# Graph attention and a routed feed-forward layer on one core: TensorE's program in loops, rows fetched by a transposing transfer, half of the rounded halves from ScalarE, small weights in three transfers

## The reference

```python
x = x + gnn(layernorm(x), adj, W, a)     # 4 heads of 32; softmax over connected nodes
x = x + ffn(layernorm(x), Wg, bg, W1, b1, W2, b2)
# gnn: h = x @ W; e = leaky_relu(s1[n] + s2[m]); attention = softmax(e where adj); attention @ h
# ffn: 8 experts of 128 -> 512 -> 128 with relu; each token goes to its 2 best by gate score,
#      weighted by the softmax of the two scores
```

## Time and profile before

| | |
|---|---|
| median of 3 runs | 625.47 us (624.49 to 626.54) |
| the profiled execution | 624.53 us, its span 622.6 us |
| mean granted TensorE clock | 0.928 |
| busy: TensorE, VectorE, ScalarE, GpSimd | 477.3, 515.9, 447.7, 402.5 us |
| line 1369, sums over neighbours | 3072 matmuls, 131.1 us |
| line 1560 and line 1543, the experts | 1704 matmuls, 107.6 us; 852 matmuls, 107.1 us |
| line 673, relu | 284 activations, 137.3 us, 0.563 each |
| line 662, copy of the transposed rows | 71 activations, 42.4 us |
| line 519, outputs written | 142 transfers, 170.1 us of GpSimd, 1.198 each |

### The profile page before, as it was taken

One profiled execution on the slowest core, in us unless ns is written; L12 is line 12 of the kernel. 1 busy time (PEld: TensorE's weight loads), 2 busy tenths in 40 slices (PEclk: granted clock), 3 DMA queues, 4 the chain that ended last, 5 costly groups with the idle time before them and its releaser, 6 DMA issues.

```text
span 622.6 us, 22344 instructions
## 1 busy us (share of the span) xinstructions
PE 477.3 (77%) x7450; PEld 435.4 (70%) x7509; DVE 515.9 (83%) x1619; ACT 447.7 (72%) x908; POOL 402.5 (65%) x342
## 2 busy tenths in 40 slices
PE   0687887977888787988867866799999999997000
PEld 0576787867888777988766755688888888887000
DVE  4689998999999999999988984678788888886297
ACT  1585778878888888998717745678888888884264
POOL 2241235887777777787776787878778887887300
PEclk9997999889989999999896998999999999999555
DMA  8922221222222233231113252233333323331499
GB/s 312 399 107 68 70 70 34 73 98 96 95 75 64 93 106 99 96 100 37 37 45 83 76 147 78 79 90 89 88 88 93 88 79 91 86 86 37 136 367 307
DMA packets 60781, 67.92 MB, mean 109 GB/s; under 512 B 7267, under 2 KB 46318, under 8 KB 60417
## 3 DMA queue, kind: packets, MB, share of 16 engines
q1 hardware_dynamic: 41936, 44.31, 22.9%
q0 software_dynamic: 8816, 17.46, 8.4%
q10 hardware_dynamic: 9920, 4.73, 2.6%
HBM read 44.16 MB, written 23.22 MB: 108 GB/s over the span
## 4 chain that ended last, share of the span: by engine, by line
issue 31%; DVE 29%; POOL 15%; PE 9%; DMA 8%; ACT 6%; POOLq 1%; SPq 1%; DVEq 0%; ACTq 0%
POOL expert_out L519 13%; PE bank L1369 4%; DVE edge L816 4%; DVE bs L719 3%; ACT xn L575 3%; DVE G L824 3%; DMA G<-in_L_ffn_W 2%; PE bank L1360 2%; DVE mv L722 2%; DMA adji<-expert_out 2%; POOL expert_rows L469 2%; DVE T L833 2%; DVE rowt L863 1%; DVE sc L759 1%; DMA G<-expert_out 1%
## 5 line engine op out<-in xcount | busy, mean ns | idle before, releaser
L519 POOL DMA_INDIRECT expert_out<-late,bidx x142 | 170.1, 1198 | 43.3 <-issue 42.7
L469 POOL DMA_INDIRECT expert_rows<-rowt,idx x128 | 156.6, 1223 | 40.6 <-issue 35.7
L570 ACT ACTIVATE G<-bank,s2c 128x512 uint8<-128x512 f32 x256 | 153.7, 703 | 0.0
L673 ACT ACTIVATE late<-bank,b1s,sc 128x256 f32<-128x256 f32 x284 | 137.3, 563 | 13.0 <-PE bank L1543 12.5
L1369 PE MATMUL bank<-V,G 128*128 128x66 bf16 x3072 | 131.1, 198 | 4.0 <-ACT G L570 0.5
L1369 PEld LDWEIGHTS bank<-V,G 128*128 128x128 fp8e4 x3072 | 121.0, 100 | 8.8 <-issue 1.6
L1560 PE MATMUL bank<-W2h,G 128*128 x1704 | 107.6, 220 | 20.2 <-DVE late L1239 18.7
L1560 PEld LDWEIGHTS bank<-W2h,G 128*128 128x128 f16 x1704 | 97.4, 98 | 36.2 <-issue 35.8
L1543 PE MATMUL bank<-late,W1h 128*128 128x256 f16 x852 | 107.1, 277 | 0.0
L1224 DVE TENSOR_TENSOR G<-late,G 128x1024 f16<-128x1024 f32 x71 | 87.0, 1226 | 2.4
L1543 PEld LDWEIGHTS bank<-late,W1h 128*128 x852 | 81.6, 99 | 9.1
(11 more groups left out here) (166 smaller groups left out, 688.9 us busy)
## 6 DMA issues: line engine op xcount, KB each, us to landing
adji<-in_adj SPq DMA_DIRECT2D x16, 1024.0 KB
V<-expert_rows SPq DMA_DIRECT2D x71, 130.0 KB
adji<-expert_out SPq DMA_DIRECT2D x8, 512.0 KB, 5.8
G<-expert_out SPq DMA_DIRECT2D x8, 512.0 KB, 8.4
expert_out<-late,bidx POOLq DMA_INDIRECT x142
G<-in_L_ffn_W SPq DMA_DIRECT2D x1, 2048.0 KB, 13.4
late<-in_L_ffn_W SPq DMA_DIRECT2D x1, 2048.0 KB, 10.1
expert_rows<-rowt,idx POOLq DMA_INDIRECT x128
```

The costliest lines, as they stand in the source:

```text
L469: pool.indirect_dma_start(xs, bass.IndirectOffsetOnAxis(ap=idx[:, Z.q, k, j:j + 1], axis=0), rowt[:, Z.q, j, :], None).then_inc(scattered[ ...
L519: pool.indirect_dma_start(ybuf, bass.IndirectOffsetOnAxis(ap=bidx[:, B.o, t:t + 1], axis=0), ysb[:, B.q, t, :], None, bounds_check=2 * TOK ...
L570: act.activation(Gs[:, M.p, h // 2, mt, :, h % 2], zb[h][:, :], ACT.Sign, bias=s2c[:, M.p, mt, h:h + 1]).then_inc(S["z_used"], 1)
L673: act.activation(h32[:, U.p, c, :], Up[U.p][c // 2][:, (c % 2) * BLK:(c % 2 + 1) * BLK], ACT.Relu, bias=b1s[:, bass.ds(ex * NC + c, 1)], s ...
```

## The change

- TensorE's slots 6 to 15 and its blocks' steps 17 to 64 run in hardware loops, two slots and eight steps per round. Waits in a loop have values computed from the loop's counter. The expert numbers come up to ten per load instead of one per block.
- SP loads a block's rows by a transposing transfer straight into `xt` (now four buffers), and the two index columns by a second transfer. TensorE's transposes, the PSUM copy on ScalarE and their semaphores go.
- ScalarE makes six activations per block: the four into `h32`, and chunks 2 and 3 once more, directly in half precision into the high half. VectorE makes the high half of chunks 0 and 1 alone, by a reduction over one element instead of a cast; the difference waits for all six.
- The small weights come in three transfers on ScalarE's queue, with W's transpose and the gate's made on the host; two transposes on TensorE and two copies go. VectorE casts most constants after the first shift. The first group's inverse deviation comes before the bias loads on GpSimd.
- `products` makes all four small products first and signals them by themselves; `scores` waits for these alone.
- Statistics of groups 2 and on come one slot later, the largest value of W1 at the end of slot 0, and the adjacency of graph 1 is loaded ahead of the rest of x.

```diff
+LOOP_SLOT = 6
+LOOP_STEP = SHARED + 1
+UNROLL = 8
+LOOPS = (BLOCKS - 2 - LOOP_STEP) // UNROLL
+REDUCED = 2
+HID_STEPS = NC + NC - REDUCED
...
             def load_rows(B):
-                ge(sp, S["bt_ready"], B.n - 3)
+                ge(sp, S["up_ready"], (B.n - 3) * NC)
                 ge(sp, S["bidx_ready"], B.n - 3)
                 r = sp.value_load(tab[0:1, 0, bass.ds(B.n, 1)], min_val=0, max_val=E * CAP)
-                sp.dma_start(xb[:, B.q], xs[bass.ds(r, BLK), :].rearrange("(t p) w -> p t w", p=P)) \
+                sp.dma_start(xt[:, B.q], xs[bass.ds(r, BLK), 0:D].bitcast(FP16), transpose=True) \
+                  .then_inc(ld_rows[B.q], 16)
+                sp.dma_start(xb[:, B.q], xs[bass.ds(r, BLK), D:ROW].rearrange("(t p) w -> p t w", p=P)) \
                   .then_inc(ld_rows[B.q], 16)
...
-            for k in range(2):
-                for h in range(H):
-                    lo = HD * (1 - k)
-                    act.dma_start(acol[HD * h:HD * (h + 1), k:k + 1],
-                                  a[h:h + 1, lo:lo + HD].rearrange("h d -> d h")).then_inc(S["ld_small"], 16)
+            act.dma_start(acol[:, :], a).then_inc(S["ld_small"], 16)
+            act.dma_start(WW[:, :, :], W).then_inc(S["ld_small"], 16)
+            act.dma_start(Wgr[:, :], Wg).then_inc(S["ld_small"], 16)
...
-                if X:
-                    act.wait_ge(S["bt_ready"], X.n + 1)
-                    ge(act, S["up_ready"], (X.n - 1) * NC)
...
-                    act.activation(xt[:, X.p], XTp(X), ACT.Copy).then_inc(S["xt_ready"], 1)
...
+                    ge(act, S["down_ready"], U.n - 3)
+                    for c in range(REDUCED, NC):
+                        act.activation(hp[:, U.q, 0, c], Up[U.p][c // 2][:, (c % 2) * BLK:(c % 2 + 1) * BLK],
                                        ACT.Relu, bias=b1s[:, bass.ds(ex * NC + c, 1)], scale=sc[:, 10:11]) \
                            .then_inc(S["hid_ready"], 1)
...
-                dve.wait_ge(S["hid_ready"], U.n * NC + NC)
+                dve.wait_ge(S["hid_ready"], U.n * HID_STEPS + REDUCED)
                 ge(dve, S["down_ready"], U.n - 3)
                 c = Chain(dve, S["split_steps"], 2, U.n)
-                c.did(dve.tensor_copy(hp[:, U.q, 0], h32[:, U.p]))
+                c.did(dve.tensor_reduce(hp[:, U.q, 0, 0:REDUCED], h32[:, U.p, 0:REDUCED].unsqueeze(3), AX.X, ALU.max))
+                dve.wait_ge(S["hid_ready"], U.n * HID_STEPS + HID_STEPS)
                 c.wait()
                 c.did(dve.tensor_tensor(hp[:, U.q, 1], h32[:, U.p], hp[:, U.q, 0], ALU.subtract))
...
                 for j in range(NT):
-                    mm(HP[:, j * P:(j + 1) * P], xnT[:, j * P:(j + 1) * P], Wr[:, :], start=True, stop=True)
                     last = mm(s12p[:, j, :], xnT[:, j * P:(j + 1) * P], Wa[:, :], start=True, stop=True)
+                last.then_inc(S["s12_ready"], 1)
+                for j in range(NT):
+                    last = mm(HP[:, j * P:(j + 1) * P], xnT[:, j * P:(j + 1) * P], WW[:, 0, :], start=True, stop=True)
                 last.then_inc(S["h_ready"], 1)
...
+            with pe.Fori(0, (NB - LOOP_SLOT) // 2) as i:
+                body(at_slot(LOOP_SLOT, i))
+                body(at_slot(LOOP_SLOT + 1, i))
...
+            def load_experts(n, where, count):
+
+                _, values = nc.values_load_multi_w_load_instructions(
+                    tab[0:1, 1, bass.ds(where, count)], engines=[pe.engine], min_val=0, max_val=E - 1,
...
-            for n in range(3, BLOCKS):
+            for n in range(3, LOOP_STEP):
+                layers(step(n))
+            pe.wait_ge(S["tab_ready"], 2)
+            with pe.Fori(0, LOOPS) as i:
+                for u in range(UNROLL):
+                    layers(looped_step(u, i))
+            rest = LOOP_STEP + LOOPS * UNROLL
+            load_experts(rest, rest, BLOCKS - rest)
+            for n in range(rest, BLOCKS):
                 layers(step(n))
```

More of the change, by code:

```diff
@@ L357, in step, with looped_step, is_block @@
         def step(n):
-            return lambda k: Batch(n + k) if 0 <= n + k < BLOCKS else None
+            at = lambda k: Batch(n + k) if 0 <= n + k < BLOCKS else None
+            at.first, at.looped, at.base = False, None, n
+            return at
+        def looped_step(u, i):
+            at = lambda k: Batch(LOOP_STEP + u + k, i, UNROLL)
+            at.first, at.looped, at.base, at.count = u == 0, i, LOOP_STEP + u, UNROLL + 2
+            return at
+        def is_block(B, n):
+            return isinstance(B.n, int) and B.n == n
         def pad_rows(eng, experts):
@@ L489, in body @@
                     scatter(m4, 0)
-                if at.s is not None and at.s + 3 < len(GROUPS):
-                    rstd1(at.s + 3)
+                if 1 <= at.s and at.s + 2 < len(GROUPS):
+                    rstd1(at.s + 2)
                 if m3 and not tail(m3):
@@ L510, in _ @@
             pool.dma_start(bgb[:, :], bg.partition_broadcast(P)).then_inc(S["small_ready"], 16)
-            for g in range(3):
-                rstd1(g)
+            rstd1(2)
             slots(pool, body, 0, NB + 1)
@@ L1120, in body @@
                 if at.s == -1:
+                    shift1(0)
+                    constants_cast()
                     group_stats(1)
-                    shift1(0)
-                    group_stats(2)
-                    dve.wait_ge(S["ld_w1"], 16)
-                    largest_weights(W1r, 0)
                 if at.s == 0:
                     shift1(1)
+                if at.s == 1:
                     shift1(2)
-                if at.s is not None and 0 < at.s <= len(GROUPS) - 3:
-                    shift1(at.s + 2)
+                if 2 <= at.s <= len(GROUPS) - 2:
+                    shift1(at.s + 1)
                 if p0:
@@ L1151, in body @@
                     arguments(p0)
+                if at.s == 0:
+                    group_stats(2)
                 if m4:
@@ L1165, in body @@
                     scaled_sums(m1, 0)
-                if at.s is not None and 0 <= at.s and at.s + 3 < len(GROUPS):
-                    group_stats(at.s + 3)
+                if 1 <= at.s and at.s + 2 < len(GROUPS):
+                    group_stats(at.s + 2)
                 if m2:
@@ L1508, in body, with at_slot @@
                     weight_rows()
-            slots(pe, body, 0, NB + 2)
-            held = [None, None, None]
-            def expert(B):
-                return pe.value_load(tab[0:1, 1, bass.ds(B.n, 1)], min_val=0, max_val=E - 1)
-            def layers(at):
-                X, U, Y = at(3), at(2), at(0)
-                if X:
-                    pe.wait_ge(ld_rows[X.q], X.f * 16 + 16)
-                    ge(pe, S["xt_ready"], X.n if X.n < SHARED else X.n - 1)
-                    if X.n == 0:
-                        pe.wait_ge(S["v_steps"], NB * X_STEPS)
-                    if X.n == SHARED:
-                        pe.wait_ge(S["xn2T_ready"], NB)
-                    xv = xb[:, X.q, :, 0:D].bitcast(FP16).rearrange("p t (q d) -> p t q d", q=2)
-                    for q in range(2):
-                        for t in range(BT):
-                            last = pe.transpose(XTp(X)[:, q, t * P:(t + 1) * P], xv[:, t, q, :], identh[:, :])
-                    last.then_inc(S["bt_ready"], 1)
-                ey, ex = held[0], held[2]
+            def at_slot(n, i=None):
+                if i is None:
+                    at = lambda k: Batch(n + k) if 0 <= n + k < NB else None
+                    at.s = n
+                else:
+                    at = lambda k: Batch(n + k, i)
+                    at.s = None
+                return at
@@ new lines, in _ @@
+            for n in range(LOOP_SLOT):
+                body(at_slot(n))
+            with pe.Fori(0, (NB - LOOP_SLOT) // 2) as i:
+                body(at_slot(LOOP_SLOT, i))
+                body(at_slot(LOOP_SLOT + 1, i))
+            for n in range(NB, NB + 2):
+                body(at_slot(n))
+            experts = {}
+            def load_experts(n, where, count):
+                _, values = nc.values_load_multi_w_load_instructions(
+                    tab[0:1, 1, bass.ds(where, count)], engines=[pe.engine], min_val=0, max_val=E - 1,
+                    skip_runtime_bounds_check_because="the table is made by this program: a count of experts below E")
+                for k in range(count):
+                    experts[n + k] = values[k]
@@ L1532, in layers @@
+            def layers(at):
+                U, Y = at(2), at(0)
+                if U and at.looped is None and U.n % GROUP == 0 and U.n <= LOOP_STEP + 1:
+                    load_experts(U.n, U.n, min(GROUP, BLOCKS - U.n))
+                if at.first:
+                    load_experts(at.base, Y.n, at.count)
+                ex, ey = [experts[at.base + k] if at(k) else None for k in (2, 0)]
                 if U:
-                    if U.n == 0:
+                    if is_block(U, 0):
                         pe.wait_ge(S["w_dve"], 2 * PIECES)
```

106 lines of the change are left out of this document (57 added, 49 removed).

## The result

The changed kernel takes 618.99 us (median of 4 runs, 618.03 to 620.85) against 624.98 (623.60 to 626.54) for the kernel before beside it: ratio 0.9912, 95% interval 0.9883 to 0.9941, that is 6.0 us less. I had said 609 and a range of 597 to 623. The profiled execution took 620.85 us, its span 619.0.

What follows compares the result with a forecast made beforehand. VectorE was taken to bound the attention slots, TensorE the expert blocks. Blocks -12.5, first blocks -3, start -2.7 and looped slots +2 summed to -16.2 us: 608.3, or 609 with the 0.9 to the median; range 597 to 623.

Steps and rivals of the forecast that it cites:

- The steady blocks: Expert blocks: period falls from 3.04 to 2.80 us, 0.24 each over 52 blocks, -12.5 us (ends -20 and 0).
- TensorE otherwise: Expert blocks: TensorE without transposes and nearly all the hole needs 2.65 to 2.95 us per block, taken as 2.75.
- ScalarE as the next bound: Expert blocks: six activations need 2.74 to 3.0 us; period 2.80, taking back half of what TensorE frees.
- GpSimd: Expert blocks: without the CAST, transfers fit 2.80, no loss; rival that GpSimd keeps 3.04, about 623.7 us, chance 0.14.
- The transposing transfer: Row loads on SP: hidden up to an issue of 1.64 us; rival that it is the bound, 672 us or 750, chance 0.09.
- First blocks: 349 to 400 us, GpSimd's scatters and sends: less blocking once the CAST goes, -3 us (0 to -6).
- Start: Kernel start: rows copied 8.3 us earlier, partly lost to the moved reduction (+3.2) and later statistics (+2.4), net -2.7 us.
- Looped slots: Attention slots 6 to 15, TensorE looped: computed waits at 0.046 us each cost +2 us in total (0 to +20).
- The price of 0.15 per wait: Rival, looped attention slots: computed waits cost 0.15 us each, 3.8 us per slot, +38, total 657 us; chance 0.06.
- Instruction stops: Rival, both TensorE loops: jumps back wait some 3 us for instruction fetches, total 625 us, or 617 if half covered; chance 0.11.
- TensorE waiting several us once per eight blocks: Expert blocks: listed among the signs that would show the prediction wrong; no size beyond several us.

Runs made afterwards that it cites:

- e1: Changed kernel with TensorE's looped expert-number load starting one entry earlier (16 + 8i) and taking twelve, the last load seven from 64: 609.68 us, ratio 0.9755 to the kernel before.
- e2: Changed kernel with the looped load still starting at 17 + 8i but taking twelve numbers instead of ten: 629.90 us, ratio 1.0080 to the kernel before.
- e5: Against the kernel with aligned loads: four ScalarE activations, all high halves by VectorE's CAST, expected to restore the 3.04 period; ratio 0.9984, repeats 1.0121, 1.0046, 0.9890, 0.9953.
- e3: Changed kernel with TensorE's attention slots 6 to 15 written out again, expert blocks still looped: 623.20 us, ratio 0.9951 to the kernel before.

## Why the prediction was wrong, step by step

The direction was right, the size was not: 6.0 us less instead of 16.

- **The steady blocks, -12.5 predicted, -3.9 measured: the failed step.** It is the sentence "three or four loads of 0.30 make 1.2. Together 1.4 per eight blocks, 0.17 per block on the sequencer, of which half may hide behind queued matmuls". The load is one of ten numbers and takes 2.54, for it starts at entry 17 + 8i; hardly any of it hides (down projections across a load are 4.92 to 5.19 apart, so 2.27 to 2.54 are lost), where I had let half of 1.4 hide. I had the row of a load of one number and took it for a price per three numbers, with nothing in the trace that said so. A round came to 23.74 us where I had 8 x 2.80 = 22.4; 1.34 over 54 / 8 rounds is 9.0 us, against the 8.6 that are missing. Shown by e1 (start moved and count raised: -9.3 us) and e2 (count alone raised: no gain). That e1 comes to 609.7, where I had said 609, is in part luck: its steady blocks gain 14.2 us, more than my 12.5, and its first blocks 0.9, less than my 3.
- **TensorE otherwise.** Between the loads it runs at 2.65, the lower end that I gave: the transposes and the hole are gone, and the computed waits add nothing to the period.
- **ScalarE as the next bound, 2.80.** Its six activations follow each other by 0.449. In the kernel after it is not the bound, since it waits for TensorE behind each stop; in e1 it sets the pace at 2.74, level with TensorE and its shorter stop. So "half of what TensorE frees is taken back" had the right engine and too much of it: with e1's loads it takes back 0.09 of the 0.39 us.
- **GpSimd.** Freed as said: 0.98 and 1.05 per block, mean 1.048 of all sends instead of 1.198 (I had said nearer 1.1). That VectorE's CAST stretches a send and the reduction doesn't is shown by lengths; I had left the second open. That the CAST's stretch and not TensorE held the 3.04 before, the theory of e5 and its repeats, no run shows; the waits of the kernel before speak against it, as did my sentence that GpSimd "isn't a second bound of equal standing".
- **The transposing transfer.** SP is held 1.22 us by it and 0.43 by the second one. That is under the 1.64 up to which I had called it hidden, and from 345 us on no engine waits for rows.
- **First blocks, -3 predicted, +0.7 measured.** The price per send was read off a mean of sends and scatters together. The scatters (16 of 42) kept their 1.24: before, two of them started inside a CAST (1.41 and 1.22 us) and three well inside a subtraction (1.53 to 1.67), after it six inside a subtraction (1.32 to 1.96), where one by itself takes 0.96. My third for the CAST left out that a transfer no longer held by it can be held by the subtraction. The sends gained 0.08 each, 27 x 0.08 = 2.1 at most. What ate that isn't settled: with the same code up to there, the stage takes 68.9 us in the kernel after, 67.4 in e1, 66.7 in e2 and 70.3 in e3, so single profiles differ by more than the gain looked for.
- **Start, -2.7.** The first scores come at 12.9 and the rows are copied at 15.7, 8.2 us earlier (I had 8.3). The connection mask of slot 1 comes 4.7 us earlier (8.3 - 3.2 = 5.1 in my sum), that of slot 6, behind the extra group of statistics, 2.9 (2.7). Right at each of these points.
- **Looped slots, +2.** The gain is 0.3 us at slot 15, so they gave back 2.6, near the +2. The price of 0.15 per wait, 3.8 us for each slot, is excluded. That it is the computed waits that cost, at 0.046 each, isn't shown: the longer slots also have the lower granted clock, and e3's shorter ones ended no earlier.
- **Instruction stops.** A jump takes 0.21 us in the blocks' loop and 0.21 to 0.24 in the slots'; the instruction queue's packets fall from 66 to 30. The mark "TensorE waiting several us once per eight blocks" did appear, and by it alone I would have called this rival right: e1, which leaves the jump alone, shows that it is the load behind the jump.

## What to carry to other kernels

Start a table load of several registers at an aligned entry, even if numbers are read that nobody uses: here it took a third of the time. The aligned starts that were run are multiples of eight; whether four is enough was not run. Work taken from each pass and collected once per round is only cheaper if its price per piece falls and nothing waits for it in one lump; behind a stop of over 2 us TensorE's granted clock sometimes fell to the lower level. And price an operation whose shape the trace doesn't show (ten numbers instead of one) from both sides: ten times the row of one was 3.0 us, and nearer the truth than my 1.2.

## What the runs showed of the hardware

- A table load on TensorE: eight numbers from entry 0, 8, 16 in 0.60 to 0.78 us, twelve from 16 + 8i in 0.85 to 0.97, seven from 64 in 1.07; ten from 17 + 8i in 2.47 to 2.65, twelve in 2.95 to 3.15, six from 65 in 1.48. That is about 0.30 for each four from an aligned start, 0.25 for each one from an odd start, and 0.25 for each of the three left over of the seven.
- A send of GpSimd takes 0.98 us by itself; one that starts inside a VectorE CAST or two-input subtraction ends 0.85 to 0.87 us after that instruction's end, one that starts inside a reduction isn't lengthened.
- ScalarE's activations back to back lengthen from 0.56 to 0.85 us in the trace while they follow each other by an unchanged 0.449: their mean (0.655 and 0.673 after, 0.563 before) is no measure of ScalarE's pace, their starts are.
- Packets rise from 60781 to 99257 from the kernel before to the one with the transposing transfer, and the DMA share in the blocks from 0.30 to 0.40; SP is held 1.22 us by each transposing transfer.
